# Batch 0's output projection, tiles 1 to 3: from fp32 matmuls to three fp32r terms, with the projection weights split one slot sooner

## The reference

```
shifted = hidden one token back
k, v = (hidden*m + shifted*(1-m)) @ Wk, Wv       r = sigmoid((...) @ Wr)
rwkv = scan over tokens, per channel: (e1*num + e2*v) / (e1*den + e2), running maximum kept
x = layernorm(x + (r * rwkv) @ Wo)               <- the output projection of this change
gate = softmax(x @ router.T) kept for the top 2 of 8 experts
x = layernorm(x + sum over experts of gate * up(silu(down(x))))
```

## Time and profile before

| | |
|---|---|
| median of 3 runs | 473.17 us |
| the profiled execution | 473.77 us, of which its span is 471.9 |
| busy share PE / DVE / ACT / POOL | 96% / 88% / 75% / 64% |
| granted TensorE clock, mean | 0.996 |
| DMA | 30.38 MB, 19% of 16 engines' time |

### The profile page before, as it was taken

How to read it: one execution, slowest core, us unless ns; L and a number is a source line. 1 busy time by engine, 2 the same in 40 slices (tenths; PEclk the granted TensorE clock), 3 DMA queues, 4 the chain that set the end, 5 groups by cost and what they waited for, 6 DMA issues and landing times. The chain is left out here.

```text
span 471.9 us, 6614 instructions
## 1 busy us (share of the span) xinstructions
PE 454.0 (96%) x1962; PEld 334.8 (71%) x1962; DVE 416.2 (88%) x620; ACT 354.7 (75%) x800; POOL 301.5 (64%) x287
## 2 busy tenths in 40 slices
PE   8999899999999999999999999999999999999993
PEld 3444566667888777877778777887778777878751
DVE  5999988899989979999899998999799997875866
ACT  1667666867787689876888778876898769768685
POOL 2354776489637987369846698279873696434335
PEclk9999999999999999999999999999999999999998
DMA  9603220023000042000420031200420012400015
GB/s 245 204 0 115 89 89 1 1 93 110 1 1 0 2 156 90 24 0 30 152 90 0 0 135 67 69 0 1 157 90 22 0 47 69 156 0 1 0 47 222
DMA packets 20100, 30.38 MB, mean 64 GB/s; under 512 B 2016, under 2 KB 7136, under 8 KB 20064
## 3 DMA queue, kind: packets, MB, share of 16 engines
q1 hardware_dynamic: 20064, 29.95, 19.4%
HBM read 21.56 MB, written 8.39 MB: 63 GB/s over the span
## 5 line engine op out<-in xcount | busy, mean ns | idle before, releaser
L560 ACT ACTIVATE PR<-PR 128x512 f32<-128x512 f32 x128 | 74.3, 581 | 29.3 <-DVE PR L858 14.9
L1150 POOL TENSOR_SCALAR NM<-SUM,RS 128x1 f32<-128x1 f32 x30 | 8.1, 271 | 106.5 <-ACT RS L560 106.5
L1144 POOL TENSOR_TENSOR DQ<-DEN,EX 128x512 f32<-128x512 f32 x32 | 41.9, 1309 | 22.2 <-DVE DEN L829 22.2
L883 DVE SCALAR_TENSOR_TENSOR KT<-D,VEC,XT 128x512 f32<-128x512 f32 x57 | 53.9, 983 | 1.2 <-POOL KL L1122 1.2
L313 PE MATMUL PV<-VH,WVH 128*128 128x512 f32 x112 | 47.7, 426 | 2.0 <-DVE NU L853 2.0
L313 PE MATMUL PK<-KH,WKH 128*128 128x512 f32 x112 | 48.1, 429 | 0.0
L317 PE MATMUL PR<-RL,WRH 128*128 128x512 f32 x112 | 45.0, 402 | 1.2 <-POOL RL L1122 1.1
L313 PE MATMUL PR<-RH,WRH 128*128 128x512 f32 x112 | 45.0, 402 | 0.8 <-POOL WRL L1175 0.6
L829 DVE TENSOR_TENSOR_SCAN DEN<-PK,EX 128x512 f32<-128x512 f32 x32 | 39.0, 1219 | 7.6 <-ACT EX L560 5.7
L317 PE MATMUL PV<-VL,WVH 128*128 128x512 f32 x112 | 44.1, 394 | 0.5 <-POOL VL L1122 0.5
L560 ACT ACTIVATE EX<-PK 128x512 f32<-128x512 f32 x32 | 19.1, 597 | 33.5 <-DVE PK L822 33.5
(11 more groups left out here) (249 smaller groups left out, 1269.1 us busy)
## 6 DMA issues: line engine op xcount, KB each, us to landing
XT<-in_xt SPq DMA_DIRECT2D x32, 256.0 KB, 3.5
XN<-in_x SPq DMA_DIRECT2D x28, 256.0 KB, 2.7
out<-XN SPq DMA_DIRECT2D x28, 256.0 KB, 2.0
X1T<-in_wo SPq DMA_DIRECT2D x1, 1024.0 KB, 5.1
XT<-in_x SPq DMA_DIRECT2D x4, 256.0 KB, 4.2
out<-XT SPq DMA_DIRECT2D x4, 256.0 KB, 2.5
X1T<-in_wk SPq DMA_DIRECT2D x2, 256.0 KB, 5.2
XN<-in_wv SPq DMA_DIRECT2D x2, 256.0 KB, 5.5
```

Source lines behind the costliest of these rows:

```text
L560: eng.activation(*a, **k).then_inc(q[s], 1)
L883: eng.scalar_tensor_tensor(out=full(b, which, c), in0=D[:, c, :], scalar=VEC[:, 2 + which, c:c + 1], in1=XT[:, c, 0:T], op0=ALU.mult, op1= ...
L1144: eng.tensor_tensor(DQ[:, :], DEN[:, 0:T], EX[:, 1, :], ALU.add).then_inc(q["e"], 1)
L1150: eng.tensor_scalar(NM1[:, col(t)], total, RS1[:, col(t)], scale, ALU.mult, ALU.mult)\
```

## The change

`FIRST` goes from 4 to 1. Tile 0 keeps its fp32 projection, tiles 1 to 3 get three terms, so ACT has three more `halve` steps and POOL three more `low_of_tile` steps, in slots 4, 5 and 6. ACT's WOH moves from the end of slot 4 to slot 3, ahead of that slot's `decay_gates(4)`. POOL's half of WOL moves from slot 5 to the end of slot 3, DVE's half from slot 5 to slot 4. Waits that named `FIRST` for another reason now name NT (4), which leaves them as they were.

```diff
-        FIRST, SPLIT = NT, NT * LAST
+        FIRST, SPLIT = 1, NT * LAST
...
# turned(t), ScalarE: the same waits as before, written with NT
-                elif t == FIRST:
+                elif t == NT:
...
# ScalarE, slot loop
+                if s == 3:
+                    eng.wait_ge(q["wo"], 16)
+                    act("woh", WOH[:, :, :], X1T[:, :, :], ACT.Copy)
                 if s < U - 1:
                     decay_gates(s + 1)
...
-                for t in now[:1] if j < 3 and 1 < b < LAST else []:
+                for t in now[:1] if j < 3 and 1 <= b < LAST else []:
                     halve(t + 1)
                 if j == 2 and batch(b + 1):
                     highs(b + 1, 1, range(2))
-                if s == C:
-                    eng.wait_ge(q["wo"], 16)
-                    act("woh", WOH[:, :, :], X1T[:, :, :], ACT.Copy)
...
# VectorE, slot loop
-                if s == C + 1:
+                if s == C:
                     eng.wait_ge(q["woh"], 1)
                     eng.tensor_tensor(WOL[:, 2:4, :], X1T[:, 2:4, :], WOH[:, 2:4, :].bitcast(F32), ALU.subtract)\
...
# GpSimd, slot loop
                 for t in now[:1]:
                     normalise(t)
-                for t in now[:1] if j < 3 and 1 < b < LAST else []:
+                for t in now[:1] if j < 3 and 1 <= b < LAST else []:
                     low_of_tile(t + 1)
                 if j == 2 and batch(b + 1):
                     lows(b + 1, 1, range(2))
-                if s == C + 1:
+                if s == 3:
                     eng.wait_ge(q["woh"], 1)
                     eng.tensor_tensor(WOL[:, 0:2, :], X1T[:, 0:2, :], WOH[:, 0:2, :].bitcast(F32), ALU.subtract)\
```

More of the change, by code:

```diff
@@ L639, in turned @@
                     eng.wait_ge(q["lo"], 3 * C * LAST)
-                elif t == FIRST:
+                elif t == NT:
                     eng.wait_ge(q["wol"], 1)
                     eng.wait_ge(q["wol1"], 1)
-                elif t and t < FIRST:
+                elif t and t < NT:
                     eng.wait_ge(q["h"], t)
-                elif FIRST + 2 <= t < NT * LAST:
+                elif NT + 2 <= t < NT * LAST:
                     eng.wait_ge(q["h"], t - 1)
```

## The result

The changed kernel takes 477.50 us, the median of 4 runs (476.56 to 477.60), beside 473.17 before (4 runs): a ratio of 1.0089, with a 95% interval of 1.0074 to 1.0104. It is slower, as forecast, and lies 0.9 us above the forecast of 476.6. In a later set of runs it took 478.34 (6 runs) beside 473.32: 1.0102 (1.0085 to 1.0120). That median lies above the upper end of the predicted range, 477.9. The profiled execution took 476.56 us with a span of 474.8, 2.9 more than the span before.

The account below looks back on a forecast made before the run. GpSimd's queue was taken to bound slots 6 to 8, PE from slot 8 on. 3.1 - 1.1 + 1.3 = 3.3 us, taken as 3.4: 473.2 + 3.4 = 476.6 us, range 474.0 to 477.9.

Parts of the forecast that it names:

- PE's saving never arrives: Tiles 1 to 3: 0.54 us of PE time saved per tile, 1.6 in all, spent waiting for GpSimd.
- WOH is hidden: ScalarE, ahead of decay_gates(4): WOH's 1.90 us fits in 2.64 us of idle time; uncovered, up to 1.9 us.
- Slot 4, 3.1 us late: Lag behind slot 4: 1.0 from late DQ, 0.4 from late WOL, 1.7 from mixes meeting differences.
- mixes meeting differences: Slots 4 to 5: GpSimd's four differences now meet all three VectorE mixes, before only the last; 1.7 us.
- turns: VectorE step with both inputs in SBUF waits for GpSimd's current step, then delays its next by about half a us.
- Slot 5 gives back 1.1: GpSimd, slot 5: tile 2's TL (1.29 us) replaces WOL (2.37), 1.08 back, so KL start 2.0 us late.
- Tile 3's TL adds 1.3: Slots 6 and 7: TL adds 1.29 us to GpSimd's closed queue; gate 3.3 late, PE 3.3 to 3.8.
- the half us: PE entering slot 8: possible extra half us, part of it coming off where PE waits again once per batch.
- No turns: Rival, slot 4: WOL and mixes keep quiet times, lag 1.0, only tile 3's TL stays; +1.3 us, 474.5; chance 0.16.
- The saving arrives: Rival, slot 7: shifted VLs avoid three or more meetings, last VL 1.2 us sooner; 472.0; chance 0.07.
- Swallowed: Rival: lag and return cancel, TL hides in GpSimd's 1.98 us idle time; within 0.5 us, 473.5; chance 0.12.
- Worse: Rival: slot 4 lag of 3.6 or more and further meetings in slot 8; 478.5; chance 0.07.

Follow-up runs that it names:

- weights_early: Changed kernel with FIRST back at 4: WOH and both WOL halves made early, all batch 0 tiles in fp32, no TL added; 474.71 us, ratio 1.0028.
- tl3_one_column: Changed kernel with GpSimd's TL of tile 3 cut to one token of 128; 475.38 and 475.46 us in two sets, ratios 1.0046 and 1.0037.
- after_again: The changed kernel run once more, unaltered, for more runs and another trace; 478.34 us, ratio 1.0102.
- wol_slot5_idle: Kernel before with GpSimd's half of WOL moved ahead of tile 1's NM in slot 5's idle time, without a wait; 473.79 us, ratio 1.0004.
- tile3_only: Kernel before with FIRST at 3: only tile 3 gets three terms, weights' rounding in its old places; 476.28 us, ratio 1.0047.

## Why the prediction was right, point by point

- **PE's saving never arrives.** Right. PE is busy 1.6 us less and waits more.
- **WOH is hidden.** Right; 0.83 of 2.64 us of idle time are left.
- **Slot 4, 3.1 us late.** The sum was right (2.98), two of its terms were not. For DQ I had 1.0 us, reading ScalarE's factor as bound by the gate alone. In the trace ScalarE's `decay_gates(5)`, which stands ahead of it, waits 1.93 us for DQ as well, and `weigh` is 2.03 late from the mark (73.76 less 55.41, against 71.99 less 55.67). My 1.0 and 0.4 (DQ and WOL) should have been 2.0, all of it from DQ: behind its WOL VectorE still waited 0.57 us for ScalarE. For mixes meeting differences I had 1.7, measured 0.95 (3.64 against 2.69): fewer turns than counted. The two errors, 0.6 too little and 0.75 too much, cancelled; that the sum came out was luck.
- **Slot 5 gives back 1.1.** Right: KL 2.01 late, 2.0 forecast. weights_early shows that more comes back where TL doesn't stand there.
- **Tile 3's TL adds 1.3.** Right: gate 3.26 late (3.3 forecast), PE 3.72 (3.3 to 3.8). tl3_one_column takes 1.08 off TL and gets 1.03 back.
- **The end.** PE comes 3.72 late into slot 8 and the span is 3.16 longer from the mark; the half us was expected to come off.
- **Size of the time.** Execution for execution the sum gave 477.2 for the profiled run, and it took 476.56 with no fall of the clock behind PE's waits. The sum had no term for such a fall. In after_again's trace it costs 1.65 us at slot 8, and the three runs at a mean clock of 0.995 or more took 476.56, 476.97 and 477.32, the other seven 477.45 to 479.90. That falls lift the median from 476.6 to 477.5 and 478.3 is likely by this, but it isn't shown run by run. The prediction also took the median as 0.6 below the profiled run, as it was before; in the first set after the change it lies 0.9 above.
- **The rivals.** "No turns" fell: `scan_den` stands at 78.54 (its sign was 77 or below), and in wol_slot5_idle a mix was held for a WOL. "The saving arrives" needed a lag behind slot 4 of under 1 us, and it is 2.98. "Swallowed" fell with tile3_only: TL stands behind the idle time. "Worse" (478.5) needed a lag of 3.6 behind slot 4, which did not come; the second set's 478.34 is close to its number, but with the same 2.98.

Left open: how much of the medians' distance is clock and how much queue, since there is one trace of each set, and why one trace with 2.49 us of waits has no fall and the other with 2.51 has one.

## What to carry to other kernels

Ask of a step that is moved into an engine's idle time not only who waits behind it in its queue, but what runs beside it on an engine that takes turns with it (here VectorE and GpSimd): here a wait that kept the two apart gained 0.9 and 1.5 us in two sets of runs, while the cheaper arithmetic, 1.6 us of PE time in three tiles, gained nothing in any kernel here. Count saved PE time only where PE is the one waited for; in a stretch bound by another engine a cheaper matmul turns into a longer PE wait. And price a longer PE wait above its length, because the clock may fall behind it, as it did in two traces of four with 2.4 to 2.5 us of waits here.

## What the runs showed of the hardware

- A VectorE step with both inputs in SBUF that starts while GpSimd is in one of its tensor steps ends some 0.5 us after that step (2.15 us beside a WOL, 0.75 alone), and GpSimd's next step is longer by about as much (1.76 instead of 1.29). The longest hold seen on one step is 1.40 us; by WOL's length it could be up to about 2.4, an estimate.
- The granted clock fell from 1.00 to 0.50 for 3.4 or 6.8 us behind PE's waits for VL (6.8 us in tile3_only, after PE had been busy 2.1 of 4 us; 3.4 us in after_again), and not in every execution of the same program. It cost 1.65 us at slot 8 in the pair of traces of the changed kernel.
